# Layer 1's first attention steps reordered: step 4's scores earlier, one norm moved from GpSimd to VectorE

## The reference

```python
x = x + _L0_xattn_ref(_layernorm(x, axis=-1), ctx_768, ...)   # 16 heads of 8, keys and values from the context
x = x + _L0_ffn_ref(_layernorm(x, axis=-1), ...)              # 8 experts, the best one for each token, relu squared
x = x + _L1_xattn_ref(_layernorm(x, axis=-1), ctx_768, ...)   # 16 heads of 8, scores clipped to +-10000
x = x + _L1_ffn_ref(_layernorm(x, axis=-1), ...)              # 8 experts, gates of the best two, gelu
```

## Time and profile before

| | |
|---|---|
| time, median of 3 runs | 239.88 us (239.61 to 239.93) |
| profiled execution | 240.54 us, of which the span is 238.8 us |
| TensorE busy | 221.9 us, 93% of the span |
| VectorE busy | 165.3 us, 69% |
| ScalarE busy | 121.7 us, 51% |
| GpSimd busy | 80.2 us, 34% |
| mean granted clock of TensorE | 0.999 |

### The profile page before, as it was taken

How to read it: one execution, slowest core, us unless ns; L and a number is a source line. 1 busy time by engine, 2 the same in 40 slices (tenths; PEclk the granted TensorE clock), 3 DMA queues, 4 the chain that set the end, 5 groups by cost and what they waited for, 6 DMA issues and landing times.

```text
span 238.8 us, 6733 instructions
## 1 busy us (share of the span) xinstructions
PE 221.9 (93%) x2534; PEld 171.7 (72%) x2534; DVE 165.3 (69%) x513; ACT 121.7 (51%) x231; POOL 80.2 (34%) x105
## 2 busy tenths in 40 slices
PE   8899988999999999999988689999799999999993
PEld 8446766776755999999886364877567786776773
DVE  1697666866455685558646765977858974799994
ACT  2555366655476556666630267656645266343340
POOL 8493300001052067756532494764800100000000
PEclk9999999999999999999999999999999999999999
DMA  6990241224004011612030310131300000001001
GB/s 204 376 406 32 72 107 53 62 80 141 3 29 134 5 34 57 168 48 77 25 77 27 90 40 9 52 90 51 92 0 4 0 0 0 3 0 47 3 0 44
DMA packets 12451, 16.38 MB, mean 69 GB/s; under 512 B 1428, under 2 KB 9620, under 8 KB 12292
## 3 DMA queue, kind: packets, MB, share of 16 engines
q1 hardware_dynamic: 10068, 12.87, 17.4%
q0 software_dynamic: 1152, 2.24, 3.2%
q10 hardware_dynamic: 1200, 0.85, 1.1%
HBM read 11.31 MB, written 3.95 MB: 64 GB/s over the span
## 4 chain that ended last, share of the span: by engine, by line
PE 75%; DVE 13%; DMA 5%; issue 3%; POOL 1%; ACT 1%; DVEq 0%; SPq 0%; ACTq 0%
PE ps L1309 12%; PE ps L1297 12%; PE ps L1088 11%; PE ps L1377 7%; PE ps L1387 7%; PE ps L997 6%; PE ps L1145 6%; DVE mx L697 4%; PE ps L1096 3%; DMA wa<-in_wa 2%; PE ps L1017 2%; DVE xn L679 2%; PE ps L1011 2%; PE ps L1053 2%; PE ps L1183 2%
## 5 line engine op out<-in xcount | busy, mean ns | idle before, releaser
L697 DVE TENSOR_REDUCE mx<-ps 128x4 f32<-128x512 f32 x64 | 41.0, 685 | 16.1 <-PE ps L1088 16.1
L522 ACT ACTIVATE PT<-ps 128x512 f32<-128x512 f32 x64 | 35.6, 590 | 24.6 <-PE ps L1096 24.6
L1088 PEld LDWEIGHTS ps<-k,q 32*128 32x128 f32 x512 | 30.9, 186 | 15.3 <-DVE mx L697 11.9
L1088 PE MATMUL ps<-k,q 32*128 32x128 f32 x512 | 36.4, 283 | 5.9 <-DVE mx L697 5.2
L1096 PE MATMUL ps<-q,k 32*128 32x128 f32 x512 | 34.9, 283 | 0.0
L1309 PEld LDWEIGHTS ps<-proj,work 128*128 128x128 f32 x256 | 30.7, 192 | 5.7 <-issue 5.7
L643 ACT ACTIVATE work<-ps,fc 128x512 f32<-128x512 f32 x32 | 21.4, 687 | 24.0 <-PE ps L1297 22.5
L1309 PE MATMUL ps<-proj,work 128*128 128x128 f32 x256 | 31.1, 275 | 0.0
L1096 PEld LDWEIGHTS ps<-q,k 32*128 32x128 f32 x512 | 29.2, 186 | 1.5 <-issue 1.3
L407 POOL DMA_INDIRECT moe_y<-ys,tok_i x22 | 22.3, 1012 | 23.6 <-DVE ys L923 11.5
L1297 PE MATMUL ps<-xT,fc 128*128 128x512 f32 x64 | 30.1, 593 | 0.0
(11 more groups left out here) (156 smaller groups left out, 316.6 us busy)
## 6 DMA issues: line engine op xcount, KB each, us to landing
proj<-in_proj SPq DMA_DIRECT2D x1, 2048.0 KB, 12.8
fc<-in_fc SPq DMA_DIRECT2D x8, 256.0 KB, 3.8
slots_x<-xs SPq DMA_DIRECT2D x2, 709.5 KB, 13.1
fc<-in_w SPq DMA_DIRECT2D x8, 129.0 KB, 2.3
proj<-in_w SPq DMA_DIRECT2D x8, 128.0 KB, 2.5
wr<-in_wr SPq DMA_DIRECT2D x1, 913.0 KB, 8.5
xs<-slots_x SPq DMA_DIRECT2D x2, 322.5 KB, 3.9
xs<-slots_x SPq DMA_DIRECT2D x2, 258.0 KB, 3.0
```

The source lines that it names most:

```text
L522: nc.scalar.activation(PT[:, j % PTR, :], ps[:, ST_BANK(layer, j), :], ACT.Exp, scale=SCALE).then_inc(b_done, 1)
L697: nc.vector.tensor_reduce(mx[:, b, 4 * g:4 * g + 4], ps[:, S_BANK(layer, j), :].rearrange("p (k m) -> p k m", m=M), axis=AX, op=ALU.max).t ...
L1088: ins = mm(ps[:, S_BANK(layer, 2 * n + i), P * k:P * k + P], q4[r:r + 32, k, L * b:L * b + L], k4[r:r + 32, k, M * b:M * b + M], start=Tru ...
```

## The change

- GpSimd no longer normalises rows 4-7; VectorE does (`ln_normalise(2, 1)`), in step 5, after the maxima of that step and the clamp of row 2.
- VectorE's statistics of rows 4-7 move from step 3 to step 4, behind that step's maxima.
- GpSimd's sum of rows 4-7 also waits for row 1's clamped maxima.
- In layer 1's step 4, TensorE issues all scores of step 4, then the transpose of row 1's maxima (which stood at the end of step 3), then row 0's transposed scores, instead of the transpose first and the two kinds of scores alternately. The idle product of step 4 goes from layer 1.
- The transposes of rows 4-7 go to bank 6 and no longer to the ring of banks 3 to 5, whose numbering has one entry less; ScalarE copies them by the ordinary `ln_evac`.
- The values of row 0 and their copy move from step 7 to the start of step 8, behind the queries of rows 4-7.

```diff
-        LN_BANK = [[4, 4], [1, 2], [0, None], [None, 6]]
+        LN_BANK = [[4, 4], [1, 2], [0, 6], [None, 6]]
...
-                if layer == 1 and n == 6:
-                    RING[1]["ln"] = len(RING[1])
...
             pool.wait_ge(gathered[1], 16)
+            pool.wait_ge(top_clip, 2)
             nc.gpsimd.tensor_tensor(xr[:, HB:B, :], xr[:, HB:B, :], yg[:, HB:B, :], ALU.add).then_inc(b_sum, 1)
             for j in range(4 * B):
                 if j == 0:
                     rsqrt(2, 1)
-                    pool.wait_ge(ln_rstd, 6)
-                    pool.wait_ge(scattered[1], 16 * HB)
-                    for b in range(HB, B):
-                        ins = nc.gpsimd.tensor_scalar(xn[:, b, 0:D], xr[:, b, :], mv[:, b, 0:1], rstd[:, b:b + 1],
-                                                      ALU.subtract, ALU.mult)
-                    ins.then_inc(ln_norm, 1)
...
                     if layer == 1 and n == 8:
                         for i in range(4, 8):
                             queries_evac_ring(i)
+                        o_evac(0)
...
                     if layer == 1 and n == 6:
-                        ln_evac_ring()
+                        ln_evac(2, 1)
...
-                    if n in O_DONE:
+                    if n in O_DONE and not (layer == 1 and n == 7):
                         o_evac(O_DONE[n])
...
                     if layer == 1 and n == 3:
                         clip_tops(1)
+                    if layer == 1 and n == 4:
                         dve.wait_ge(b_sum, 1)
                         ln_stats(2, 1)
...
                     if layer == 1 and odd and b < B and b != 1:
                         clip_tops(b)
+                    if layer == 1 and n == 5:
+                        ln_normalise(2, 1)
...
                 if layer == 1 and n == 6:
-                    pe.wait_ge(b_done, ring_no(1, "ln") - 3)
-                    pe.wait_ge(ln_norm, 6)
-                    for i in range(4):
-                        ins = nc.tensor.transpose(ps[:, ring_at(1, "ln"), 128 * i:128 * i + 128], xn[:, 4 + i, 0:D], ident[:])
-                    ins.then_inc(ln_tr, 1)
+                    ln_transpose(2, 1)
...
             def second_queries():
-                pe.wait_ge(b_done, ring_no(1, "ln"))
+                pe.wait_ge(ln_xT, XT_NO(2, 1))
...
                     if layer == 1 and n == 8:
                         second_queries()
+                        for j in range(4):
+                            values(j)
                     if n < 2 * B:
                         scores(n)
-                    if 0 <= m < 2 * B:
+                    alone = layer == 1 and m == 0
+                    if 0 <= m < 2 * B and not alone:
                         scores_t(m)
                     for k in range(4):
                         for i in range(2):
                             if n < 2 * B:
                                 score(n, i, k)
                         for i in range(2):
-                            if 0 <= m < 2 * B:
+                            if 0 <= m < 2 * B and not alone:
+                                score_t(m, i, k)
+                    if alone:
+                        top_transpose(1)
+                        scores_t(m)
+                        for k in range(4):
+                            for i in range(2):
                                 score_t(m, i, k)
...
-                    if n == 3:
+                    if layer == 0 and n == 3:
                         top_transpose(1)
-                    if n in (4, 5):
+                    if n == 5 or layer == 0 and n == 4:
                         pe.wait_ge(v_sb, 2)
                         idle_product(256)
...
-                    for u in VALUE_UNITS.get(n, ()):
+                    for u in VALUE_UNITS.get(n, ()) if (layer, n) != (1, 7) else ():
                         values(2 * u)
                         values(2 * u + 1)
```

## The result

The changed kernel took 241.63 us in the middle of 20 executions (239.91 to 242.49), the kernel before 239.89 (239.51 to 242.26, also 20). The ratio is 1.0043, with a 95% interval of 1.0023 to 1.0063. (The two medians differ by 1.74 us or 0.73%, the two means by 0.97 us or 0.40%: the ratio of two kernels whose executions fall into groups depends on which is taken.) An execution over 1.5% above the fastest of its kernel is left out of a ratio, though not of a median; none of these 40 is. I had forecast 240.0, and a range up to 240.9. The middle lies above it.

The account below looks back on a forecast made before the run. In the changed stretch it took the chain through VectorE and GpSimd, not TensorE, as the bound. Step 5 earlier (-0.87), norms (+1.47) and values behind queries (-0.42) gave +0.18, so 240.0 us, range 238.3 to 240.9.

Parts of the forecast that it names:

- -0.87: Start of step 5: its scores start at 135.65 instead of 136.52, 0.87 us earlier.
- +1.47: Between steps 6 and 7: VectorE's norms turn 0.87 us earlier into 0.6 later, costing 1.47 us.
- -0.42: Step 7 to step 8: values behind the queries take 5.6 us instead of 6.02, saving 0.42.
- The step that decided: VectorE's norms of rows 4-7: one done per GpSimd clamp, the last at about 140.95.
- the lower bound: VectorE's four norms run freely beside GpSimd's clamps, 1.11 us for four, done at 139.4.
- the upper bound: VectorE's norms held through a GpSimd sum and clamps, ending about 1.1 us beyond 140.95.
- it lay in a wait and returns nothing: Step 4 on TensorE: dropping the idle product of 256 columns changes the time by nothing.
- 0.04 is for something else: Whole kernel: a chance of 0.04 left for any outcome outside the named cases.
- The second: VectorE's norms run freely beside the clamps, step 8 starts at 145.75: 238.5 us, chance 0.25.
- The third: A norm on VectorE loses its turn to GpSimd's 1.09 us sum, last norm at 142.0: 241.1 us, chance 0.10.
- fourth: Clamps and norms never overlap, each norm costs 0.87 us, last at 142.15: 241.2 us, chance 0.06.

Follow-up runs that it names:

- r2_after_again: The changed kernel run again without an edit on another chip, against the kernel before: 240.35 us, ratio 1.0006.
- e7: The changed kernel with GpSimd's clamps held until VectorE's four norms are done and step 4's idle product put back: 238.48 us, 0.9934 of before.
- e1c: The changed kernel with two idle products of 512 columns added in step 6 ahead of the transposes of rows 4-7: 240.24 us, 1.0020 of before.
- e8_less_idle: The changed kernel with the idle product of layer 1's step 5 also taken away: 241.62 us, 1.0082 of before.
- r1_after_again: The changed kernel run again without an edit on a slower chip, against the kernel before: 248.85 us, ratio 0.9975.
- r4_after_again: The changed kernel run again without an edit on another slower chip, against the kernel before: 248.61 us, ratio 1.0002.

## Why the prediction was wrong

**The order: right, with the hundredths by luck.** The sum was -0.87, +1.47, -0.42, in all +0.18. Without a fall the profile has +0.18 (r2_after_again), of these terms: -0.91, +1.37, -0.28. Step 7 came 0.14 sooner than forecast; step 7 to step 8 took 5.74 us instead of 5.6, since the query products took 3.63 us up to the values (142.05 to 145.68) where the forecast had 3.44. The errors cancel, and the 20.70 that they are taken against is known to 0.2. The step that decided was right: that VectorE gets one norm done for each clamp was taken from the last group of rows, and it measured 2.44 for four, done at 141.0 (140.95 forecast). Freed, it is 1.11, the lower bound; the upper bound, a lost turn, was not seen.

**The step that failed: the clock.** The prediction has no term for TensorE's clock; it prices all products at the full one. It says of step 4's idle product that "it lay in a wait and returns nothing", and it puts four transposes behind a norm that ends at 140.95 without counting how long TensorE stands before them. That was in its own numbers: scores of step 6 from 137.67 for 1.10 us end at 138.8, so TensorE has some 2 us with nothing but one transpose, where its longest idle time in these steps was 1.51. "0.04 is for something else" held the case that came. In the profiled execution step 7's scores took 1.53 us (141.66 to 143.19) instead of 1.10 and the query products 4.91 instead of 3.70, together 1.64 longer, which is the whole of +1.81 less +0.18. Eleven further executions had a mean clock of 0.986 to 0.993 and took 241.42 us or more, and the six at 1.000 stand at 239.98 in the middle, on the forecast. That the median came out of the range is so also a matter of the chip: on two others it was 240.35 and 239.97, inside the range.

**The rivals.** The second (norms run freely, 1.4 below before) describes what e7 reached by another means, 1.49 below in the profile; that its 238.48 us are the rival's 238.5 is chance, since before took 240.22 on that chip. The third and fourth did not occur: no norm lost a turn for a whole sum, and the six clamps kept 3.50 us.

**What stays open.** What makes the clock fall in one execution and not in the next is not known, nor why costly ones are 12 of 20 on the first chip and 7 of 24 on two others. The five profiles of the changed kernel show a fall in step 7 once, one from step 5 on twice, and none twice. That the 2.04 us are what lets the costly one come is likely by its place and by the 5 of 24 with them filled, and not shown: e1c still had 4 of 12. The first comparison's +1.7 us in the middle is explained by its executions (239.98 in the middle for those at full clock, 241.91 for the others), but only one of the fourteen was profiled, and two of them took no longer than those without a fall.

## What to carry to other kernels

When a change moves work between engines, add up how long TensorE now stands in each place, beside the time of the steps: idle products that seem to lie in a wait may hold the clock. Here the removal of one in step 5 cost 1.65 us in the middle, while one put back in step 4 gave nothing that could be measured. Before an operation from SBUF to SBUF is moved to VectorE, look at what GpSimd does at that moment; four norms took 1.11 us alone and 2.44 beside clamps, and letting GpSimd wait for them, where the clamps had time, took the changed kernel from the level of before to 0.7% below it. Of a kernel whose executions fall into groups, read the granted clock of each before looking for a cause in the order, and profile more than one: the mean says that the clock fell, not where, and the place decided what it cost.

## What I had not expected of the hardware

The clock fell behind idle times of 0.77 and 0.81 us in steps 4 and 5 (e8_less_idle), shorter than the 2.04 that left it at full speed in r2_after_again and than the 1.51 of before. A single idle time is thus no guide here; what else decides, these runs don't show. A fall that comes early is cheaper than one in the query products: with 6.8 us at half the clock (136.9 to 143.7), e8's time from step 0 to step 8 was 21.96 us (125.98 to 147.94), less than the 22.51 of the changed kernel with 3.4. It met waits, and GpSimd's clamps, which then came with breaks, let the norms through in 1.80. In r1_after_again and r4_after_again, with 3.4 us at half the clock from step 5 on, the stretch was even shorter (20.49 and 20.50 us) than with no fall at all (20.88).
